# Two stacked axial attention layers in fp32: group statistics on the vector engine instead of TensorE, and the batch loop turned round

## The reference

```python
x = x + _L0_conv_ref(_gn(x), w_qkv0, w_out0, w_qkv1, w_out1)
x = x + _L1_conv_ref(_gn(x), Wq, bq, Wk, bk, Wv, bv, Wo, bo, sigma)

def _gn(v, G=32, eps=1e-05):
    g = v.reshape(B_, H_, W_, G, C_ // G)
    m = jnp.mean(g, axis=(1, 2, 4), keepdims=True)
    s = jnp.var(g, axis=(1, 2, 4), keepdims=True)
    return ((g - m) / jnp.sqrt(s + eps)).reshape(v.shape)

# L0: attention without softmax, 16 heads of 16 channels, once along columns (axis 0) and once along rows (axis 1)
qkv = x @ w_qkv
dots = jnp.einsum('bhie,bhje->bhij', q, k) * d ** (-0.5)
out = jnp.einsum('bhij,bhje->bhie', dots, v)
return out.transpose(0, 2, 1, 3).reshape(b, t, d) @ w_out

# L1: one head of 256 channels, softmax along rows and along columns with a distance term
r_attn = jax.nn.softmax(einsum('bhwd,bhkd->bhwk', q, k) - gw[0] * _dist(w), axis=-1)
c_attn = jax.nn.softmax(einsum('bhwd,bgwd->bwhg', q, k) - gw[0] * _dist(h), axis=-1)
return jnp.einsum('bhwd,ed->bhwe', r_out + c_out, Wo) + bo
```

## Time and profile before

| what | value |
|---|---|
| median of 3 runs | 242.77 us (239.31 to 244.72) |
| the profiled execution's own time | 239.23 us |
| its span, first to last instruction | 237.1 us |
| mean granted TensorE clock | 0.985 of full |
| busy: PE / DVE / ACT / POOL | 223.7 / 164.2 / 130.1 / 71.5 us |
| PE weight loads, beside its matmuls | 194.1 us |
| bytes moved by DMA | 13.97 MB, mean 59 GB/s |

### The profile page before, as it was taken

One profiled execution on the slowest core, in us unless ns is written; L12 is line 12 of the kernel. 1 busy time (PEld: TensorE's weight loads), 2 busy tenths in 40 slices (PEclk: granted clock), 3 DMA queues, 4 the chain that ended last, 5 costly groups with the idle time before them and its releaser, 6 DMA issues.

```text
span 237.1 us, 8176 instructions
## 1 busy us (share of the span) xinstructions
PE 223.7 (94%) x3264; PEld 194.1 (82%) x3264; DVE 164.2 (69%) x494; ACT 130.1 (55%) x321; POOL 71.5 (30%) x102
## 2 busy tenths in 40 slices
PE   7899999999999999999999999999999999994884
PEld 6557888789989898889888998989888988882772
DVE  5797694787558775778468755877577846676463
ACT  2556642665646773666556564677366655734341
POOL 6400170316412443316431641234331643003000
PEclk9999999999999999999999999999999999999589
DMA  6962101230023202340125002410122012300002
GB/s 215 365 150 49 50 0 28 48 108 3 6 55 104 61 0 41 51 129 0 23 52 146 0 6 51 125 40 0 39 50 88 0 22 53 105 3 0 0 3 88
DMA packets 16030, 13.97 MB, mean 59 GB/s; under 512 B 3600, under 2 KB 15504, under 8 KB 16016
## 3 DMA queue, kind: packets, MB, share of 16 engines
q1 hardware_dynamic: 14480, 11.88, 19.6%
q10 hardware_dynamic: 1536, 1.90, 2.4%
HBM read 7.47 MB, written 2.10 MB: 40 GB/s over the span
## 4 chain that ended last, share of the span: by engine, by line
PE 88%; DVE 4%; ACT 3%; issue 2%; POOL 1%; POOLq 0%; DVEq 0%
PE bank L963 52%; PE bank L1048 7%; PE bank L1026 7%; PE bank L1237 5%; PE bank L1057 3%; PE bank L970 3%; PE bank L980 2%; ACT kv L408 1%; PE bank L1102 1%; PE bank L1384 1%; PE bank L985 1%; PE bank L976 1%; PE bank L1404 1%; PE bank L1146 1%; PE bank L1346 1%
## 5 line engine op out<-in xcount | busy, mean ns | idle before, releaser
L397 ACT ACTIVATE k_v<-bank 128x512 f32<-128x512 f32 x32 | 19.0, 597 | 32.8 <-PE bank L963 29.5
L320 POOL TENSOR_TENSOR rstd<-var_eps,minus_half 128x2 f32<-128x2 f32 x16 | 11.3, 704 | 85.3 <-DVE var_eps L635 85.3
L408 ACT ACTIVATE kv<-bank,head_scale 128x256 f32<-128x256 f32 x64 | 25.1, 480 | 4.7 <-PE bank L1026 4.7
L311 POOL TENSOR_TENSOR xt_lo<-xn,xn_hi 128x256 fp32r<-128x256 f32 x14 | 18.7, 1359 | 20.2 <-DVE xn_hi L644 20.2
L389 ACT ACTIVATE xn<-bank,nbias,rstd 128x256 f32<-128x256 f32 x28 | 14.3, 562 | 16.1 <-DVE nbias L640 16.0
L652 DVE TENSOR_TENSOR kv<-bank,block_mask 128x512 f32<-128x512 f32 x32 | 20.5, 683 | 1.8 <-PE bank L1026 1.6
L1048 PE MATMUL bank<-kv,q 64*32 64x128 f32 x1024 | 18.4, 273 | 2.1 <-DVE kv L652 0.5
L614 DVE BATCH_NORM_STATS2 moments<-bank 128x6 f32<-128x256 f32 x32 | 12.2, 422 | 9.7 <-PE bank L970 7.8
L1026 PE MATMUL bank<-v_wide,k_v 64*32 64x128 f32 x1024 | 18.5, 273 | 0.1
L1048 PEld LDWEIGHTS bank<-kv,q 64*32 64x32 f32 x1024 | 14.4, 105 | 4.8 <-issue 4.8
L418 ACT ACTIVATE o_even<-bank,parity 128x256 f32<-128x256 f32 x32 | 13.5, 477 | 8.0 <-PE bank L1048 8.0
(11 more groups left out here) (229 smaller groups left out, 698.2 us busy)
## 6 DMA issues: line engine op xcount, KB each, us to landing
v_wide<-k_v SPq DMA_DIRECT2D x122, 32.0 KB, 2.0
x_res<-in_x_dram SPq DMA_DIRECT2D x8, 256.0 KB, 2.9
x_in<-in_x_dram SPq DMA_DIRECT2D x7, 256.0 KB, 3.1
out_dram<-y_out SPq DMA_DIRECT2D x7, 256.0 KB, 2.9
wqkv_in<-in_L_conv_w_qkv_dram SPq DMA_DIRECT2D x2, 384.0 KB, 5.9
wqkv_in<-in_L_conv_w_qkv_dram ACTq DMA_DIRECT2D x2, 384.0 KB, 7.1
wl<-in_L_conv_Wk_dram ACTq DMA_DIRECT2D x1, 256.0 KB, 3.5
wl<-in_L_conv_Wq_dram SPq DMA_DIRECT2D x1, 256.0 KB, 3.9
```

The lines of the kernel that those rows point to most:

```text
L311: pool.tensor_tensor(xt_lo[:, c, :].rearrange("p (w h) -> p w h", w=SIDE), by_axis(xn[0][:, c, :], 0), by_axis(xn_hi[0][:, c, :].bitcast(F ...
L397: act.activation(k_v[:, axis, t, :, :].rearrange("p i d -> p (i d)"), src[:, :], ACT.Copy).then_inc(kv_taken, 1)
L408: last = act.activation(kv[axis][:, 1, :, :, :, head // 2, own].rearrange("p t c s e -> p (t c s) e"), kv_bank[1][:, :].rearrange("p (a e) ...
```

## The change

Four things change together.

1. Group statistics. `group_avg` and the two matmuls per norm are gone. DVE transposes the per-channel moments in 32 x 32 blocks, sums over 8 neighbours, and transposes the coefficients back. PSUM bank 1 becomes free.
2. The first norm (k = 0) runs two entries ahead instead of one: `transpose_x(b+2)`, `statistics(0, b+2)`, `normalise(0, b+2)`, `split_xn(0, b+2)` and POOL's `turn(b+2)` stand in pass b. The q, k, v projections of entry b+1 move up by one place each: `project_kv(b+1, 1)` before `transpose_output(b, 0)`, `project_kv(b+1, 3)` before x1 is transposed, `project_q(b+1, 1)` before `key_value(b+1, 1)`.
3. Other banks: x is transposed into bank 1, `project_q(.., 1)` writes bank 0, the weighted values bank 1.
4. The loop covers b = 1 to 5; entry 6 is written out without the work for an entry 8, and the last entry has another order: the rest of layer L1 of entry 6 is moved behind layer L0 of entry 7, done in plain fp32 in buffers of its own, and `keep_busy` puts dummy matmuls on PE at three places there.

The core of the diff, first on DVE:

```diff
-            def spread(k, b):
-                dve.wait_ge(stat_sum[k], 2 * b + 1)
-                dve.tensor_copy(gmean[k][:, :], stat_bank[:, 0:CC]).then_inc(norm_step[k], 1)
...
-            def variance(k, b):
-                dve.wait_ge(stat_sum[k], 2 * b + 2)
-                dve.tensor_scalar(var_eps[k][:, :], stat_bank[:, CC:2 * CC], EPS, None, ALU.add).then_inc(var_ready[k], 1)
+            def group_variance(k, b):
...
+                dve.transpose(turned_mv[k][:, 0:2, :], mv[k][:, :, :]).then_inc(norm_step[k], 1)
...
+                dve.tensor_reduce(group_sum[k][:, :], turned_mv[k][:, 0, :].rearrange("p (g i) -> p g i", g=GROUPS), AX.X, ALU.add
...
+                dve.scalar_tensor_tensor(off_mean[k][:, :].rearrange("p (g i) -> p g i", g=GROUPS),
...
+                dve.tensor_tensor(turned_mv[k][:, 2, :], off_mean[k][:, :], off_mean[k][:, :], ALU.mult).then_inc(norm_step[k], 1)
...
+                dve.tensor_reduce(square_sum[k][:, :], turned_mv[k][:, 1:3, :].rearrange("p s (g i) -> p g s i", g=GROUPS), AX.XY, ALU.add
...
+                dve.tensor_scalar(var_eps[k][:, :], square_sum[k][:, :], 1.0 / GROUP, EPS, ALU.mult, ALU.add).then_inc(var_ready[k], 1)
             def coefficients(k, b):
                 dve.wait_ge(rstd_ready[k], b + 1)
-                dve.scalar_tensor_tensor(nbias[k][:, :], gmean[k][:, :], -1.0, rstd[k][:, :], ALU.mult, ALU.mult).then_inc(coef_ready[k], 1)
+                dve.scalar_tensor_tensor(rstd_nbias[k][:, 1, :], group_sum[k][:, :], -1.0 / GROUP, rstd_nbias[k][:, 0, :], ALU.mult, ALU.mult
...
+                dve.transpose(coef[k][:, :, :], rstd_nbias[k][:, :, :].unsqueeze(3).broadcast_to([P, 2, GROUPS, GROUP])
...
+            def attention(b, far):
+                take_odd(b, 1)
+                low_t(b - 1)
+                mask_kv(b, 0)
...
+                split_o(b, 1)
+                maxima(b - 1)
+                if far:
+                    statistics(0, b + 2)
+                    group_variance(0, b + 2)
+                split_o(b, 0)
+            def project(b, far):
+                invert_sums(b - 1)
+                if far:
+                    coefficients(0, b + 2)
+                add_residual(b)
+                if far:
+                    dve.wait_ge(kv_proj, TILES * (b + 1) + TT)
+                    split_xn(0, b + 2)
                 statistics(1, b)
...
+                group_variance(1, b)
+                split_attn(b - 1)
                 coefficients(1, b)
...
+                mask_kv(b + 1, 1)
+                final_sum(b - 1)
                 split_xn(1, b)
```

On ACT:

```diff
+            def project(b, far):
+                take_kv(b + 1, 2)
+                if far:
+                    normalise(0, b + 2)
+                take_kv(b + 1, 3)
+                split_attn(b - 1)
+                if not far:
+                    place_rest(b + 1)
+                take_q(b + 1, 1)
+                mask_kv(b + 1, 1)
                 normalise(1, b)
```

On POOL:

```diff
+            def batch(b, far):
+                if far:
+                    inverse_root(0, b + 2)
+                weights(b - 1)
+                inverse_root(1, b)
+                if far:
+                    turn(b + 2)
+                add_bias(b)
```

On PE:

```diff
-                pe.matmul(stat_bank[:, 0:CC], group_avg[:, :], mv[k][:, :, 0], start=True, stop=True).then_inc(stat_sum[k], 1)
-                pe.matmul(stat_bank[:, CC:2 * CC], group_avg[:, :], shift[k][:, 0, :], start=True, stop=True).then_inc(stat_sum[k], 1)
+            def attention(b, far):
+                queries(b, 1)
+                project_t(b - 1)
+                key_value(b, 0)
+                project_values(b - 1, 0)
+                project_values(b - 1, 1)
+                queries(b, 0)
...
                 transpose_output(b, 1)
+                if far:
+                    transpose_x(b + 2)
+                project_kv(b + 1, 0)
...
+                project_q(b + 1, 0)
...
+                project_kv(b + 1, 1)
                 transpose_output(b, 0)
...
                 project_out(b, 1)
+                project_kv(b + 1, 2)
                 project_out(b, 0)
+            def project(b, far):
+                project_kv(b + 1, 3)
+                transpose_x1(b)
...
+                transpose_weights(b - 1)
...
+                project_q(b + 1, 1)
+                key_value(b + 1, 1)
+                if far:
+                    pe.wait_ge(xn_ready[0], b + 3)
+                weighted_values(b - 1, 0)
+                weighted_values(b - 1, 1)
...
+            with pe.Fori(1, LAST - 1) as b:
+                attention(b, True)
+                project(b, True)
+            attention(LAST - 1, False)
+            project(LAST - 1, False)
```

More of the change, by code:

```diff
@@ L34 @@
 GROUP = 8
+SQUARE = 32
+GROUPS = SQUARE // GROUP
 EPS = 1e-5
@@ L276, in batch @@
                     place_v(b + 1, 1)
-                    place_v(b + 1, 0)
+                    place_v(b + 1, 0, range(SEQS if next_batches >= 2 else BY_SYNC))
                     next_residual(b + 1)
@@ L371, in _ @@
             inverse_root(1, LAST)
+            for t in range(TT):
+                pool.wait_ge(late_inverse, t + 1)
+                pool.tensor_tensor(attn[:, t, :], exp_col[:, t, :], inv_sum[:, 1, t:t + 1].broadcast_to([P, TOKENS]), ALU.mult)
+                pool.tensor_tensor(row_weights[:, t, :], exp_row[:, t, :], inv_sum[:, 0, t:t + 1].broadcast_to([P, P]), ALU.mult
+                                   ).then_inc(soft_step, 1)
+                pool.wait_ge(soft_step, LAST + t)
+                own = attn[:, t, t * P:(t + 1) * P]
+                last = pool.tensor_tensor(own, row_weights[:, t, :], own, ALU.add)
+            last.then_inc(attn_ready, 1)
         @block.scalar
@@ L877, in _ @@
             low_out()
-            make_mask(2)
-            split_o(0, 0)
-            project(0, False, True)
-            with dve.Fori(1, BATCHES - 1) as b:
-                attention(b, True, True)
-                project(b, True, True)
+            statistics(0, 2)
+            group_variance(0, 2)
+            split_o(0, 0)
+            coefficients(0, 2)
+            add_residual(0)
+            dve.wait_ge(kv_proj, TILES + TT)
+            split_xn(0, 2)
+            statistics(1, 0)
@@ L903, in _ @@
             statistics(1, LAST, last_x_bank)
-            invert_sums(LAST - 1)
-            spread(1, LAST)
-            variance(1, LAST)
-            dve.wait_ge(soft_step, LAST)
-            for t in range(TT):
-                own = attn[:, t, t * P:(t + 1) * P]
-                last = dve.scalar_tensor_tensor(own, exp_row[:, t, :], inv_sum[:, 0, t:t + 1], own, ALU.mult, ALU.add)
-            last.then_inc(attn_ready, 1)
+            group_variance(1, LAST)
+            late_logits(0)
             coefficients(1, LAST)
+            late_maxima(0)
             dve.wait_ge(coef_ready[1], BATCHES)
+            dve.wait_ge(s_ready, TT * LAST)
             dve.tensor_scalar(xn[1][:, 1, :], last_x_bank[1][:, TOKENS:2 * TOKENS], rstd[1][:, 1:2], nbias[1][:, 1:2],
@@ L1071, in project_out, with project_t @@
                     last.then_inc(y_ready, 1)
-            def project_t(b):
+            def project_t(b, halves=range(CC)):
                 pe.wait_ge(xn_split[1], b + 1)
-                for m in range(CC):
+                for m in halves:
                     last = product(t_bank[:, m * TOKENS:(m + 1) * TOKENS],
@@ L1313, in _ @@
             project_q(1, 0)
+            pe.wait_ge(o_lo_done, 1)
+            project_kv(1, 1)
             transpose_output(0, 0)
+            transpose_x(2)
             pe.wait_ge(w_split, 3)
@@ L1406, in _ @@
                 last.then_inc(last_pv_ready, 1)
+            values(LAST, 0)
+            pe.wait_ge(last_t_taken, 2)
+            plain_scores(0, t_last, last_s_bank[0][:, 0:TOKENS])
+            pe.wait_ge(row_done, TT * LAST)
+            values(LAST, 1)
+            plain_scores(1, t_last, last_s_bank[1][:, 0:TOKENS])
+            keep_busy(4)
+            pe.wait_ge(attn_ready, LAST)
+            for j in range(TT):
+                for i in range(TT):
+                    last = pe.transpose(late_at_bank[:, (j * TT + i) * P:(j * TT + i + 1) * P], attn[:, i, j * P:(j + 1) * P], ident[:, :])
+            last.then_inc(at_ready, 1)
+            keep_busy(2)
+            pe.wait_ge(last_v_taken, TT)
+            pe.wait_ge(row_done, TT * BATCHES)
+            last_transpose(0)
+            pe.wait_ge(late_at_taken, 1)
+            late_weighted_values(0)
+            last_weighted_values(0)
+            last_transpose(1)
+            late_weighted_values(1)
+            last_weighted_values(1)
 _INS = ['x', 'L0_conv_w_qkv0', 'L0_conv_w_out0', 'L0_conv_w_qkv1', 'L0_conv_w_out1', 'L1_conv_Wq', 'L1_conv_bq',
```

554 lines of the change are left out of this document (259 added, 295 removed).

## The result

The changed kernel takes 249.25 us (median of 4 runs, 248.37 to 249.58). The kernel before takes 243.25 us (median of 4, 239.31 to 244.72). The ratio is 1.034, with a 95% interval of 1.020 to 1.047: slower. The forecast was 241.7 us with a range of 233.5 to 248.0, so the time lies outside it. The profiled execution took 249.27 us, with a span of 247.5 us; forecast was a span of 236.1. Some executions of a kernel run one or two per cent longer at a lower granted clock; the ratios here leave them out, the medians do not.

A forecast was written before the change was run, and what follows sets the result against it. PE's own instruction stream was taken to bound the loop. Ahead of the loop +1.9, passes +2.0, last pass -0.4 and tail -4.5 gave -1.0: span 236.1, time 241.7 us, range 233.5 to 248.0.

The forecast's parts named there:

- Place C: From the end of `key_value(b+1, 1)` to `project_t(b)`: 4.0 us, with only 2.56 us of PE work to put there.
- The road over DVE: From x1 transposed through statistics, group variance, power, coefficients, mask and final sum to the split: 5.6 us.
- Place A: From `project_t`'s start to `queries(b, 0)`: stays at 4.75 us, with a PE stall of 0.5.
- place B: From `queries(b, 0)` to the end of `key_value(b+1, 1)`: 17.35 us of PE work, inputs arriving in time.
- group variance: The six new DVE steps per norm that replace the matmul averages: 1.35 us.
- Five passes, +2.0: The loop: five passes, each 26.1 us instead of 25.70, add 2.0 us.
- Ahead of the loop, +1.9: Before the loop: `queries(1, 1)` starts at 49.2 us instead of 47.31, adding 1.9.
- Last pass, -0.4: The written-out last pass loses x transposed and its statistics: 0.4 us less than its 24.3 so far.
- Tail, -4.5: From `queries(7, 1)` to the end: shorter road to the output product, full clock at the end; 4.5 us less.
- PE alone sets the pass: Rival, 20%: PE's 24.2 us of work sets each pass, so the whole takes 230.6 us.
- The statistics chain is longer: Rival, 14%: statistics on DVE and POOL cost 0.9 us more per norm, nine times; 250.0 us.
- The clock falls again: Rival, 16%: half clock in the tail or PE's wait ahead of the loop, +2.4 us; 244.2 us.

The follow-up runs named there:

- e1: The changed kernel, with POOL waiting for the second norm's coefficients before it turns the entry two ahead; 245.56 us, ratio 1.020.
- e2: The changed kernel, with POOL waiting until the second norm's split is done before it turns the entry two ahead; 241.53 us, ratio 1.001.
- e5: The kernel before, with an unused POOL add of two tiles behind each second norm's power; 245.0 us, ratio 1.016.
- e11: e10, but ahead of the loop POOL turns entry 2 only after the vector engine's first t_lo; 234.53 us, ratio 0.980.
- e8: The changed kernel without the 14 dummy matmuls of its tail; 249.21 us, ratio 1.032.
- e4: The kernel before with the group statistics on DVE, order and tail kept, three more dummy matmuls ahead of the loop; 241.07 us, ratio 1.002.
- e10: The changed kernel with POOL's turns held back, final sum, transposes, x load and first mask reordered, a PE wait moved, more dummy matmuls; 237.09 us, ratio 0.977.

## Why the prediction was wrong

- **Place C, the step that failed.** "The road over DVE is then 5.6 us to the split; that over ACT is [...] 5.6 too. They tie, so any more on DVE's side adds to the pass." I had counted each step at its time beside a still POOL, and never asked where the reordering puts POOL's `turn(b + 2)`. It stands right behind the power, so it runs during the coefficients, and `add_bias` during the split. Price: 0.93 + 0.41 us in each of five passes, shown by e1, e2 and, from the other side, e5. The sign was in the trace of before, one of 16 and beside POOL's x1b:

```profile
L640 DVE SCALAR_TENSOR_TENSOR nbias<-gmean,rstd x16: 149/160/680, 8.6 to 219.4; 128x2 f32<-128x2 f32 x16
43.82 0.68 DVE L640 SCALAR_TENSOR_TENSOR nbias<-gmean,rstd 128x2 f32<-128x2 f32 x1 [0.80 <-POOL rstd L320]
43.75 1.42 POOL L349 TENSOR_TENSOR x1b<-x,bias_out 128x256 f32<-128x256 f32 x2
```

It was even in a row that I used. L817 in the earlier trace rows took 0.71 us from 33.40 on, beside the end of this, and 0.35 in the changed kernel:

```profile
31.74 2.23 POOL L314 CAST xt_hi<-xn_hi 128x256 fp32r<-128x256 f32 x2
```

- **The sum.** The span came out 11.4 us over the forecast (247.5 against 236.1): about 1.3 ahead of the loop, 7.4 in the five passes, 2.3 in the last pass, 0.6 in the tail. The time missed by only 7.5 us, because a second error hid 3.5 of it: the factor 1.015 from the profiled execution to the median, read from the kernel before, was 1.000 here (249.25 against 249.27).
- **Place A (4.75 forecast, 4.81), place B (17.35, 17.3), group variance (1.35, 1.38)**: right. With POOL out of the way, e2 has the forecast pass of 26.1 us and the forecast place C (4.01 against 4.0). Two terms of its road over DVE were off and nearly cancel: the power on four columns takes 1.02 us instead of 0.70, and the steps behind it overlap at their ends by most of that. That e2's time agrees as well (241.53 against 241.7) is luck. Its span is 241.9 us against 236.1: 51.33 ahead of the loop (forecast 49.2), 131.68 for five passes (130.5), 25.65 for the last (25.0) and 33.26 for the tail (31.3); and its profiled execution, at 243.71, lies above its median and not 1.5% below.
- **Five passes, +2.0.** They took, with the first, 137.87 us from 50.48 to 188.35, against 5 x 26.1 = 130.5: +7.4, of which 6.8 is 1.37 a pass. The first pass is 0.7 us longer than the others and holds the half-clock stretch from 51 to 54 us, which is likely the rest.
- **Ahead of the loop, +1.9.** It was +3.2: `queries(1, 1)` at 50.48, not at 49.2. L874, four columns beside POOL's turn, took 0.63 where the same step takes 0.15 in e11, and the clock was at half from 27 to 30 us. In the other direction the mask's four steps, counted at 1.96 from the earlier trace rows, took 1.59 (45.78 to 47.37). How the rest divides is not shown.
- **Last pass, -0.4.** 27.29 us instead of 25.0. It has xn_lo's stall (0.41) at its start, and 3.4 us at half clock from 191 to 194, behind PE's waits of 1.45 and 0.85 us, which I estimate at 1.7.
- **Tail, -4.5.** 31.86 us instead of 35.76, -3.9; the mean clock is 1.00. Right within 0.6. That the plain matmuls and the dummies hold the clock was argued: e2 has both and falls in its tail all the same, and e8 leaves the dummies' part open.
- **The rivals.** "PE alone sets the pass" is out: PE is idle for 2.85 us of it. "The statistics chain is longer" gave 250.0 us, near the result, but with other parts: of its two terms the transpose was wrong (0.24, not 0.4) and the power half right (1.02, not 1.2), which makes about 0.4 us a norm where that rival needed 0.65, and e4 shows that the chain alone costs no time in the whole. "The clock falls again" came true in another place: three stretches of 3.4 us in the profiled execution, by estimate 1.7 us each, 5.1 in all, against 3.6 us for the 7.2 at half in the earlier trace rows. That is 1.5 of the 10 us between the two profiled executions. For the 6.0 us between the medians no such part is shown: the kernel before has a mean clock of 0.979 in the execution at its median on e1's chip (242.15 us), and the changed kernel 0.979 to 0.986. Two of the three stretches follow waits of PE, but the passes in between have waits of 1.57 and 0.72 us and no fall, so what makes it fall is not shown.

By this account the change itself, the statistics on DVE and the loop turned round, is worth nothing in time (e2: 1.001), and the 6 us were lost to where POOL's work came to stand beside DVE's. The way from e2 to e10 shows that the turned loop did open room: 0.6 us a pass, once final sum, transposes and the load of x were put in their places.

## What to carry to other kernels

When a change moves work, list for each moved wait what the engines off the critical path will run at that moment, not only when they finish: here POOL's turn and bias add, which nobody waited for (e2 holds them back until the split is done and loses nothing), cost 1.34 us a pass by running beside two steps of DVE. The sign in a profile is one instruction form with a longest duration far over its median (1092 ns against 163), and its end just behind the end of an instruction of another engine; the cure is a wait that keeps the idle engine idle a little longer. And a move that is free by itself (the final sum) can be charged by the next (the transposes) over a queue that neither names: SP's.
